# Causal attention by pairs of query tiles, with the values as the stationary operand

## The reference

```
def _L3_attn_ref(x, Wq, Wk, Wv):
    ...
    q = jnp.einsum('btc,hc->bth', x, Wq)
    k = jnp.einsum('btc,hc->bth', x, Wk)
    v = jnp.einsum('btc,hc->bth', x, Wv)
    scores = jnp.einsum('bth,bsh->bts', q, k) * Cd ** (-0.5)
    causal = jnp.tril(jnp.ones((Td, Td), dtype=bool))
    scores = jnp.where(causal, scores, -jnp.inf)
    attn = jax.nn.softmax(scores, axis=-1)
    out = jnp.einsum('bts,bsh->bth', attn, v)
    return out
...
    t = t + _L3_attn_ref(_ln_t(t), L3_attn_Wq, L3_attn_Wk, L3_attn_Wv)
```

## Time and profile before

| | |
|---|---|
| median of 3 executions | 3429.18 us |
| the profiled execution | 3425.23 us |
| its span in the trace | 3423.2 us |
| granted clock of TensorE, mean | 0.951 of full speed |
| TensorE busy over the span | 3109.1 us, 91% |
| the causal attention, from the end of the normalisation ahead to the last matmul | 2511.7 to 3174.4 us |

### The profile page before, as it was taken

One profiled execution on the slowest core, in us unless ns is written; L12 is line 12 of the kernel. 1 busy time (PEld: TensorE's weight loads), 2 busy tenths in 40 slices (PEclk: granted clock), 3 DMA queues, 4 the chain that ended last, 5 costly groups with the idle time before them and its releaser, 6 DMA issues. The chain is left out here.

```text
span 3423.2 us, 60243 instructions
## 1 busy us (share of the span) xinstructions
PE 3109.1 (91%) x23425; PEld 2431.8 (71%) x23425; DVE 1828.6 (53%) x3657; ACT 1276.4 (37%) x2435; POOL 1056.2 (31%) x1104
## 2 busy tenths in 40 slices
PE   6999996788865989999999999999889998999799
PEld 4777774333523478888888888888768886888555
DVE  5566675477525345555555555555245554555365
ACT  2555553211222244444444444444033333333200
POOL 3455450477321054444444444453000000000000
PEclk9999997899976999999999999999589999999799
DMA  7988850000011355455554554552100000000000
GB/s 174 193 183 177 180 151 2 13 1 1 1 61 65 126 86 78 70 76 79 74 78 72 75 81 65 84 75 43 58 6 1 1 1 1 1 1 1 8 20 30
DMA packets 407108, 213.32 MB, mean 62 GB/s; under 512 B 313972, under 2 KB 386316, under 8 KB 405036
## 3 DMA queue, kind: packets, MB, share of 16 engines
q1 hardware_dynamic: 388960, 199.27, 30.7%
q10 hardware_dynamic: 17868, 10.19, 1.4%
HBM read 177.82 MB, written 52.89 MB: 67 GB/s over the span
## 5 line engine op out<-in xcount | busy, mean ns | idle before, releaser
L1670 DVE TENSOR_TENSOR sl_vl_slot<-sl_psV_slot,sl_vh_slot 128x512 fp32r<-128x512 f32 x1024 | 636.0, 684 | 564.2 <-ACT sl_vh_slot L1649 564.2
L1649 ACT ACTIVATE sl_vh_slot<-sl_psV_slot 128x512 fp32r<-128x512 f32 x1024 | 529.3, 604 | 584.8 <-PE sl_psV_slot L1617 584.7
L85 PE MATMUL sl_psY_slot<-sl_vl_slot,sp_Mh_sp 128*128 128x256 f32 x2048 | 604.0, 295 | 0.0
L86 PE MATMUL sl_psY_slot<-sl_vh_slot,sp_Ml_sp 128*128 128x256 f32 x2048 | 577.8, 282 | 0.0
L87 PE MATMUL sl_psY_slot<-sl_vh_slot,sp_Mh_sp 128*128 128x256 f32 x2048 | 576.8, 282 | 0.0
L85 PEld LDWEIGHTS sl_psY_slot<-sl_vl_slot,sp_Mh_sp 128*128 128x128 f32 x2048 | 389.1, 190 | 91.1 <-issue 90.6
L86 PEld LDWEIGHTS sl_psY_slot<-sl_vh_slot,sp_Ml_sp 128*128 128x128 f32 x2048 | 390.4, 191 | 0.0
L87 PEld LDWEIGHTS sl_psY_slot<-sl_vh_slot,sp_Mh_sp 128*128 128x128 f32 x2048 | 389.7, 190 | 0.0
L1593 POOL CAST sl_fh_slot<-sl_f_slot 128x512 fp32r<-128x512 f32 x256 | 167.3, 654 | 576.2 <-PE sl_psV_slot L1617 576.2
L1595 POOL TENSOR_TENSOR sl_fl_slot<-sl_f_slot,sl_fh_slot 128x512 fp32r<-128x512 f32 x256 | 337.8, 1319 | 20.6
L1860 PE MATMUL ca_ps_ca<-ca_v_ca,ca_pt_ca 128*128 128x128 f32 x2112 | 284.3, 280 | 25.5 <-ACT ca_pt_ca L1949 14.2
(11 more groups left out here) (382 smaller groups left out, 5542.8 us busy)
## 6 DMA issues: line engine op xcount, KB each, us to landing
sl_f_slot<-filt_hat SPq DMA_DIRECT2D x256, 256.0 KB, 5.5
na_v_na<-na_windows SPq DMA_DIRECT2D x128, 390.0 KB
na_windows<-na_values SPq DMA_DIRECT2D x160, 113.8 KB, 6.7
na_values<-na_vo_na ACTq DMA_DIRECT2D x32, 260.0 KB, 7.3
u_hat<-fw_o_fwd SPq DMA_DIRECT2D x8, 1024.0 KB, 3.8
sl_u_slot<-u_hat SPq DMA_DIRECT2D x128, 64.0 KB, 2.2
y_hat<-sl_y_slot SPq DMA_DIRECT2D x128, 64.0 KB, 4.7
X<-in_x SPq DMA_DIRECT2D x8, 512.0 KB, 7.9
```

Source lines behind the costliest of these rows:

```text
L85: e.matmul(out, lh, rl, start=start, stop=False)
L86: e.matmul(out, ll, rh, start=False, stop=False)
L1649: e.activation(v_out(0, n, q), bank(4 * n + q), ACT.Copy).then_inc(S["v_high"], 1)
L1670: e.tensor_tensor(v_out(1, n, q), bank(m), v_out(0, n, q), ALU.subtract).then_inc(S["v_split"], 1)
```

## The change

The layer becomes one block without a loop over the batches; both are written out one after the other. Queries go by pairs of tiles: `P` counts the 32 pairs of both batches, p = P % 16 is the pair's place in its batch, and `m` counts the steps of a pair. A step (P, m) covers two key tiles: PE turns up to 2x2 tiles of 128x128 into one bank, and multiplies with each key tile of v as the stationary operand and the 256 columns of both query tiles of `ca_pt` as the moving one. The output comes with the channels in the partitions, as X has it, and the turning back falls away. To scale it, PE spreads the reciprocals over the partitions by a matmul with the identity (L1918 in the new file), ACT copies them, and DVE multiplies and adds.

The projections stand between the steps: `project(P + 1)` computes k and v of 512 tokens for every other pair and q of 256 tokens for each. The scores of pair P + 1 are spread over steps of pair P by `scored`, as one to six products a step. Projected inputs, scores and reciprocals share a ring of four banks (`ring`, `slot`). ACT takes the exponential chunk by chunk, up to 512 columns, by the list `early`: at step (P, m) the chunk m + 2 of the pair itself, and in the last two steps the first two of the next pair, ahead of the step's copy; for the pairs with p < 3 the first two of the next pair come at the pair's end (`late`). One row of every second pair is kept in the part of Y that has been projected. The copy of a turned bank goes to ACT in even steps and to DVE in odd ones, and `values(g - 2)` stands behind `turn(g)`.

```diff
@@ -1744,212 +1744,321 @@
...
-        with nc.Fori(0, B) as b:
-            with P.block() as block:
...
+        ALL = B * PAIRS
+        steps = [(P, m) for P in range(ALL) for m in range(P % PAIRS + 1)]
+        first = {P: g for g, (P, m) in enumerate(steps) if m == 0}
+        end = lambda P: first[P] + P % PAIRS
+        copied = lambda g: (S["pt_dve"] if g % 2 else S["pt_act"], g // 2 + 1)
+        ends_at = lambda g: steps[g][1] == steps[g][0] % PAIRS
...
+        def row(P, t, a, n):
+            b = P // PAIRS
+            if P % 2 and t:
+                return Y[:, b * L + a:b * L + a + n]
+            return rows[P % 2][t][:, a:a + n]
+        chunks = lambda P: P % PAIRS // 2 + 1
+        width = lambda P, t, x: min(CH, (2 * (P % PAIRS) + 1 + t) * 128 - x * CH)
+        def prepares(P, m):
+            return P + 1 < ALL and m == (PAIRS // 2 if P % PAIRS == PAIRS - 1 else 0)
+        def scored(P, m):
+            p = P % PAIRS
+            if P + 1 == ALL or m < 0:
+                return 0
+            n = 2 * chunks(P + 1)
+            if p == PAIRS - 1:
+                return n if m >= p - 3 else 0
+            if p < 3:
+                return n if m == p else 0
+            return min(n, -(-n * m // (p - 2)))
+        def early(P, m):
+            own = range(m + 2, min(m + 3, 2 * chunks(P)))
+            ahead = m - P % PAIRS + 1
+            following = range(ahead, ahead + 1) if P + 1 < ALL and P % PAIRS >= 3 and ahead >= 0 else range(0)
+            return [(P, i) for i in own] + [(P + 1, i) for i in following]
+        late = lambda P, m: P + 1 < ALL and P % PAIRS < 3 and m == P % PAIRS
...
+            @block.tensor
+            def _(e):
+                def ring(key):
+                    n = slot[key]
+                    if n >= NS:
+                        e.wait_ge(S["s_taken"], n - NS + 1)
+                    return psS[n % NS]
...
+                def scores(P, a, n):
+                    if a < n:
+                        e.wait_ge(S["s_taken"], slot["k", kv_pair(P)] + 1)
+                        e.wait_ge(S["s_taken"], slot["q", P] + 1)
+                    for i in range(a, n):
+                        t, x = divmod(i, chunks(P))
+                        k = width(P, t, x)
+                        product(e, ring(("s", P, i))[:, 0:k], [q[:, t * 128:(t + 1) * 128] for q in q_in],
+                                [kk[:, x * CH:x * CH + k] for kk in k_all], True, True).then_inc(S["s_in_psum_c"], 1)
+                def turn(g):
+                    P, m = steps[g]
+                    p = P % PAIRS
+                    e.wait_ge(S["exp_done_c"], piece[P, 2 * (m // 2) + 1] + 1)
+                    if g >= 2:
+                        e.wait_ge(*copied(g - 2))
+                    for j in range(2):
+                        for t in range(2):
+                            if m == p and j == 1 and t == 0:
+                                continue
+                            at = 256 if m == p and j == 1 else j * 256 + t * 128
+                            tr = e.transpose(psT[g % 2][:, at:at + 128], row(P, t, (2 * m + j) * 128, 128), T["ident"][:, :])
+                    tr.then_inc(S["t_in_psum_c"], 1)
...
+                def values(g):
+                    P, m = steps[g]
+                    p = P % PAIRS
+                    out = psO[P % 2]
+                    e.wait_ge(*copied(g))
+                    e.wait_ge(S["s_taken"], slot["v", kv_pair(P)] + 1)
+                    if m == 0 and P >= 2:
+                        e.wait_ge(S["s_taken"], slot["r", P - 2] + 1)
...
+                    elif m == p:
+                        weigh(out[:, 128:256], 2 * m + 1, 256, 128, False, False)
+                        mm = weigh(out[:, :], 2 * m, 0, 256, False, True)
+                    else:
+                        for j in range(2):
+                            mm = weigh(out[:, :], 2 * m + j, j * 256, 256, m == 0 and j == 0, False)
+                    mm.then_inc(S["pv_done"], 1)
+                    if m == p:
+                        e.wait_ge(S["ri_done_c"], P + 1)
+                        bank = ring(("r", P))
+                        for t in range(2):
+                            mm = e.matmul(bank[:, t * 128:(t + 1) * 128], ri[:, P % 2, t:t + 1].to_broadcast([128, 128]),
+                                          T["ident"][:, :], start=True, stop=True)
+                        mm.then_inc(S["s_in_psum_c"], 1)
+                e.wait_ge(S["ca_loaded"], 32)
+                project(0)
+                scores(0, 0, 2)
+                for g, (P, m) in enumerate(steps):
+                    turn(g)
+                    if g >= 2:
+                        values(g - 2)
+                    if prepares(P, m):
+                        project(P + 1)
+                    scores(P + 1, scored(P, m - 1), scored(P, m))
+                values(len(steps) - 2)
+                values(len(steps) - 1)
...
+                def project(P):
+                    b, p = divmod(P, PAIRS)
+                    if p % 2 == 0:
+                        at = p // 2 * CH
+                        e.activation(k_all[0][:, at:at + CH], take(("k", P))[:, :], ACT.Copy).then_inc(S["high_done_c"], 1)
+                    e.activation(q_in[0][:, :], take(("q", P))[:, 0:PW2], ACT.Copy, scale=scale).then_inc(S["high_done_c"], 1)
+                def exponentials(P, i):
+                    x, t = divmod(i, 2)
+                    e.wait_ge(S["nmax_done"], 2 * P + t + 1)
+                    if i < 2 and P >= 2:
+                        e.wait_ge(S["ri_done_c"], P - 1)
+                    part = row(P, t, x * CH, width(P, t, x))
+                    e.activation(part, part, ACT.Exp, bias=nm[:, P % 2, t:t + 1], accum_out=rs[:, P % 2, t, x:x + 1])\
+                        .then_inc(S["exp_done_c"], 1)
+                def copy_turned(g):
+                    P, m = steps[g]
+                    n = 384 if m == P % PAIRS else CH
+                    e.wait_ge(S["t_in_psum_c"], g + 1)
+                    if g >= 3:
+                        e.wait_ge(S["pv_done"], g - 2)
+                    e.activation(pt[g % 3][:, 0:n], psT[g % 2][:, 0:n], ACT.Copy).then_inc(S["pt_act"], 1)
...
+                project(0)
+                for i in range(2):
+                    exponentials(0, i)
+                for g in range(len(steps) + 2):
+                    if g < len(steps):
+                        P, m = steps[g]
+                        for Q, i in early(P, m):
+                            exponentials(Q, i)
+                        if g % 2 == 0:
+                            copy_turned(g)
+                    if g >= 2 and ends_at(g - 2):
+                        copy_reciprocals(steps[g - 2][0])
+                    if g < len(steps):
+                        if prepares(P, m):
+                            project(P + 1)
+                        if late(P, m):
+                            for i in range(2):
+                                exponentials(P + 1, i)
...
+                def project(P):
+                    b, p = divmod(P, PAIRS)
+                    if p % 2 == 0:
+                        at = p // 2 * CH
+                        e.wait_ge(S["high_done_c"], high["k", P] + 1)
+                        e.tensor_tensor(k_all[1][:, at:at + CH], psS[slot["k", P] % NS][:, :], k_all[0][:, at:at + CH], ALU.subtract)\
+                            .then_inc(S["s_taken"], 1)
+                        e.wait_ge(S["s_in_psum_c"], slot["v", P] + 1)
+                        e.tensor_copy(v_all[:, at:at + CH], psS[slot["v", P] % NS][:, :]).then_inc(S["s_taken"], 1)
+                    e.wait_ge(S["high_done_c"], high["q", P] + 1)
+                    e.scalar_tensor_tensor(q_in[1][:, :], psS[slot["q", P] % NS][:, 0:PW2], scale, q_in[0][:, :], ALU.mult, ALU.subtract)\
+                        .then_inc(S["s_taken"], 1)
...
+                def reciprocals(P):
+                    e.wait_ge(S["exp_done_c"], piece[P, 2 * chunks(P) - 1] + 1)
+                    e.tensor_reduce(total[:, P % 2, :], rs[:, P % 2, :, 0:chunks(P)], AX.X, ALU.add).then_inc(S["sums_done"], 1)
+                    e.wait_ge(S["sums_done"], P + 1)
+                    if P >= 2:
+                        e.wait_ge(S["s_in_psum_c"], slot["r", P - 2] + 1)
+                    e.reciprocal(ri[:, P % 2, :], total[:, P % 2, :]).then_inc(S["ri_done_c"], 1)
+                def finish(P):
+                    b, p = divmod(P, PAIRS)
+                    x = X[:, b * L + p * PW2:b * L + (p + 1) * PW2]
+                    e.wait_ge(S["r_copied"], P + 1)
+                    e.wait_ge(S["pv_done"], end(P) + 1)
+                    e.tensor_tensor(r_sb[:, :], psO[P % 2][:, :], r_sb[:, :], ALU.mult).then_inc(S["s_taken"], 1)
+                    e.wait_ge(S["s_taken"], slot["r", P] + 1)
+                    e.tensor_tensor(x, r_sb[:, :], x, ALU.add).then_inc(S["x_added_c"], 1)
+                e.wait_ge(S["ca_loaded"], 32)
+                project(0)
```

(52 more changed lines are left out.)

249 lines of the change are left out of this document (68 added, 181 removed).

## The result

The changed kernel takes 3389.13 us (median of 4 runs, 3382.18 to 3393.25), the kernel before 3429.7 us beside it. The ratio is 0.9863, 95% interval [0.9847, 0.9880]: 1.4% faster, 40.6 us by the medians. Run again beside other kernels it came to 0.9856 [0.9841, 0.9871] and 0.9868 [0.9841, 0.9895]. The forecast was 3392 us, range 3372 to 3412, with 0.90 on faster.

What follows compares the result with a forecast made beforehand. PE's in-order work plus stops and half clock was taken to bound the layer. Terms summed to 628.4 us against 662.7, giving 3390.9 from the profiled 3425.2; with the median 4 us above the profiled run, 3392 us, range 3372 to 3412.

Steps and rivals of the forecast that it cites:

- Entry: Start of the layer: without the second block the first matmul starts earlier, 3.9 us instead of 5.4.
- PE's work: All PE instructions of both batches: 581.6 us before, values 6.1 less, output 7.3 more, so 582.8 after.
- Stops that go: Row ends, where values waited for copies of the last turns: about 0.51 us at 62 rows, 32 us gone.
- Exponentials hidden: ACT in the steps: 224 extra exponentials, 105 us more on ACT, hidden behind PE; 3 us allowed at pair ends.
- Stops at pairs 1 to 4: Chained starts of the small pairs in each batch: PE stops for 9.1 us a batch, 18.2 in all.
- Clock: Half clock at the batch starts: costs 8 us in the first batch and 2.5 in the second.
- Bare loads and switches: PE: loads bared at some 20 stops, 2 us; full precision to fp32r and back in some 160 steps, 4 us.
- the first (small pairs cost more): Rival, chance 0.14: small-pair chains grow to 15 us a batch, the clock costs 18 us; 3412 us.
- The second (stops hide better): Rival, chance 0.12: DVE and ACT run ahead, most hand-overs shrink to 1 us, wide matmuls take 0.211; about 3374 us.
- The third: Rival, chance 0.02: weight loads set the pace of the value matmuls, 122 us instead of 230; 3284 us.
- The fourth: Rival, chance 0.07: ACT's 136 copies come late behind exponentials, 0.90 us bare in each; about 3480 us, deciding at 0.25 a copy.
- The fifth: Rival, chance 0.03: DVE's `finish` blocks the ring of four banks at each pair, 1.1 us at 32 pairs; no change, 3427 us.

Runs made afterwards that it cites:

- narrow run: Changed kernel with 480 of its 510 wide value matmuls of 256 columns split into two of 128; 3405.07 us, 0.9896 of the kernel before.
- kernel with late values: Kernel before, with only the values of a row's last piece moved behind the next row's first turns, output and scaling a row later; 3399.20 us, 0.9877.
- two kernels with more load on ACT: Changed kernel with one or three unneeded ACT copies of 512 columns ahead of each of its 136 ACT copies; 3382.91 us (0.9870) and 3406.93 us (0.9908).
- reordered kernel: Changed kernel with the next pair's products ahead of the older values at the ends of pairs 0 to 2, reciprocals' copy and finish later; 3371.27 us, 0.9840.

## Why the prediction was right

By its own terms, with the layer from the end of the normalisation to the last addition, 628.4 said and 618.6 measured:

- *Entry*: 3.9 said, 4.3 measured.
- *PE's work*: 582.8 said; counts by the measured paces (216 ns wide, 112 and 109 narrow, 229 a product's instruction) are 581.3. The values gain 8 us from width, said 6; the narrow run shows that.
- *Stops that go*: 32 said. The kernel with late values shows 29, and about 5 us of half clock with them, which the prediction had booked under the clock and the turnover.
- *Exponentials hidden*: right. The two kernels with more load on ACT show room, and the allowance of 3 us for tight pair ends was not needed. Its step "with its read 0.47 us ... 105 us more on ACT" was mis-sized: it added durations that overlap. By starts an exponential of 512 is 0.71 us, so 0.28 of it fixed, 224 x 0.28 = 63 us; the page's ACT time grew by 61.8 (1276.4 to 1338.2).
- *Stops at pairs 1 to 4*: 18.2 said. By starts, 8.1 us in the first batch (0 to 1: 1.40 for q and 2.23, 1 to 2: 2.47, 2 to 3: 2.00) and 7.6 in the second; the one from 3 to 4 does not exist: 15.7. The first chain 2.8, said 2.6.
- *Clock*: 10.5 said. At half are 2517.8 to 2522.0, 2525.5 to 2535.7, 2542.5 to 2545.9 and 2846.3 to 2849.7; less the stops inside, and halved, 8.8 us.
- *Bare loads and switches*: 2 + 4 said, 4.0 left over. The switch costs nothing: behind a wide value the product's first instruction starts 0.68 us after four values, 0.19 early, and the second 0.41 later, 0.18 late (3068.25 to 3069.34, above). The 4.0 are what the other terms leave of the layer: an unexplained remainder.
- *Tail*: 1.4 said, 1.6 measured.

Together 4.3 + 581.3 + 15.7 + 2.8 + 8.8 + 4.0 + 1.6 = 618.5, which closes because the remainder is in it. No term was off by more than 3 us, and nearly all errors had one sign, so the layer came out 9.8 us shorter than said. That the time lies within 3 us of the forecast is in part luck: the profiled run, at 3382.18 us, is 8.7 below the 3390.9 that the sum gave for it, and the median of the four happens to lie 7 above that run.

Of the rivals, the first (small pairs cost more) didn't come: 8.1 and 7.6 us of stops a batch against its 15, and 8.8 for the clock against its 18. The second (stops hide better) describes half of the miss: the 3 to 4 stop and the pair ends vanished, though the other starts did not shrink to 1 us. The third is refuted by the 216 ns. The Trainium skill's figures in "TensorE: Matmul & The Clock Gate", section Back-to-back issue gap, gave an estimate of 98 ns there; neither the trace nor the narrow run agrees for these full-precision matmuls. The fourth's point of decision, 0.25 us a copy on ACT, was far too near: 0.6 more a copy cost 3 us in all. The fifth's `finish` can have cost something at one place only, ahead of pair 2's scores: the reordered kernel made of the 2.47 us stop from 1 to 2 two pieces, 0.85 for q and 0.87 for the exponential, but it moved the values there as well. In the steady part no product waits at all.

One reason was incomplete. The prediction said that `values(g - 2)` leaves each copy a step and so removes the stops. True of the copies, but one step is enough for them, and both the second step of lag and the values carried over a pair's end serve another chain, that of q.

## What to carry to other kernels

Where PE works in order and a copy stands between its turns and its values, look at what lies between the two at the ends of the loop first: carrying one piece of values across the end of a row gave four fifths of what the whole rewriting gave in this layer. Cost ACT by the distance of starts, not by durations, before calling it tight. And after such a change read the first pairs of each batch again: what is left to gain (another 14 us here, 3.5 of them from earlier loads and about half of the rest with the clock) is at the starts, not in the steady part, in which PE is busy in all of 273.70 us.
